# The second form of the attention rounds in a scan, attention and expert decoder layer: centred values, decays with the gate as bias, scores ahead of values

## What is computed

```python
log_fg = log_sigmoid(fg); cs = cumsum(log_fg)
log_D = where(lower triangle, cs - cs.T, -inf) + ig.T
D = exp(log_D - max(log_D))
C = (qh @ kh.T / sqrt(32)) * D
normalizer = maximum(abs(sum(C)), exp(-max_log_D))
h = (C / (normalizer + 1e-6)) @ vh
out = (h - mean(h)) * rsqrt(var(h) + 1e-5) * outnorm_scale     # over the 32 of a head
x = layernorm(x + out)
```

## Time and profile before

| | us |
|---|---|
| median of 3 runs | 702.19 |
| the three runs | 701.72, 706.64, 702.19 |
| the profiled execution | 706.54 |
| its span, first to last instruction | 704.9 |

### The profile page before, as it was taken

One profiled execution on the slowest core, in us unless ns is written; L12 is line 12 of the kernel. 1 busy time (PEld: TensorE's weight loads), 2 busy tenths in 40 slices (PEclk: granted clock), 3 DMA queues, 4 the chain that ended last, 5 costly groups with the idle time before them and its releaser, 6 DMA issues.

```text
span 704.9 us, 10813 instructions
## 1 busy us (share of the span) xinstructions
PE 544.6 (77%) x3387; PEld 386.7 (55%) x3387; DVE 430.6 (61%) x880; ACT 329.5 (47%) x732; POOL 369.7 (52%) x301
## 2 busy tenths in 40 slices
PE   2589999899889888686384889797878689989800
PEld 0234434445344447675263768686667568988800
DVE  1599999999999941676748376656352612211155
ACT  2475685876867553122132435444443323333327
POOL 1497979999789752216506163625253533322341
PEclk9999999999999995555555789998898899999955
DMA  4434535444454532732341735361616157788594
GB/s 148 148 101 148 175 122 166 146 170 167 137 179 146 191 74 52 133 62 62 77 113 42 193 120 158 136 232 36 203 63 216 59 177 243 241 292 270 170 244 117
DMA packets 83319, 104.51 MB, mean 148 GB/s; under 512 B 40784, under 2 KB 64592, under 8 KB 83136
## 3 DMA queue, kind: packets, MB, share of 16 engines
q1 hardware_dynamic: 74576, 90.99, 42.4%
q0 software_dynamic: 4320, 8.92, 3.7%
q10 hardware_dynamic: 4368, 3.93, 2.0%
HBM read 91.48 MB, written 12.34 MB: 147 GB/s over the span
## 4 chain that ended last, share of the span: by engine, by line
PE 25%; issue 24%; POOL 20%; DVE 10%; DMA 9%; ACT 3%; SPq 2%; another core or an unknown queue 1%; POOLq 0%; ACTq 0%; DVEq 0%
POOL hc L640 12%; PE pB L1063 7%; PE pq L1076 4%; DMA wslot<-in_expert_w 4%; PE py L818 4%; PE py L1063 2%; POOL y_dram L745 2%; PE pC L997 1%; ACT x_all L1457 1%; DMA y_dram<-dx,xin 1%; PE pa L979 1%; POOL xg_dram L736 1%; DMA x_all<-y_dram 1%; POOL bcs L604 1%
## 5 line engine op out<-in xcount | busy, mean ns | idle before, releaser
L640 POOL TENSOR_TENSOR hc<-h,Crep 128x1024 f32<-128x1024 f32 x64 | 149.7, 2356 | 14.6 <-DVE h L1507 13.2
L745 POOL DMA_INDIRECT y_dram<-dx,xin x71 | 68.9, 971 | 153.9 <-ACT dx L1378 144.8
L1063 PE MATMUL pB<-Crep,wslot 128*128 128x256 f32 (+1 forms) x556 | 118.9, 360 | 21.9 <-DMA wslot<-in_expert_w 10.7
L818 PE MATMUL py<-hc,ident 128*128 128x512 f32 x256 | 120.7, 598 | 8.1 <-POOL hc L640 8.1
L1063 PEld LDWEIGHTS pB<-Crep,wslot 128*128 128x128 f32 x556 | 90.8, 204 | 38.7 <-DMA wslot<-in_expert_w 14.0
L1498 DVE TENSOR_TENSOR u<-dx,pC 128x1024 f32<-128x1024 f32 x64 | 77.3, 1207 | 17.4 <-PE pC L807 17.3
L818 PEld LDWEIGHTS py<-hc,ident 128*128 128x128 f32 x256 | 46.8, 189 | 53.9 <-issue 37.4
L1789 DVE TENSOR_TENSOR Crep<-u,pB 128x512 f32<-128x512 f32 x35 | 24.0, 686 | 85.5 <-PE pB L1063 42.2
L1507 DVE TENSOR_TENSOR_SCAN h<-pB,u 128x1024 f32<-128x1024 f32 x32 | 73.1, 2285 | 1.0 <-ACT pB L1196 0.6
L1507 DVE TENSOR_TENSOR_SCAN h<-pa,u 128x1024 f32<-128x1024 f32 x32 | 73.1, 2284 | 0.0
L1789 DVE TENSOR_TENSOR u<-u,pB 128x512 f32<-128x512 f32 x36 | 24.8, 688 | 78.9 <-PE pB L1063 46.0
(11 more groups left out here) (225 smaller groups left out, 952.0 us busy)
## 6 DMA issues: line engine op xcount, KB each, us to landing
wslot<-in_expert_w SPq DMA_DIRECT2D x46, 768.0 KB
Crep<-c_dram SPq DMA_DIRECT2D x64, 512.0 KB, 3.8
h<-m_dram SPq DMA_DIRECT2D x16, 256.0 KB
xin<-xg_dram SPq DMA_DIRECT2D x25, 130.0 KB
cT_st<-in_ctx_T SPq DMA_DIRECT2D x8, 256.0 KB, 4.1
dx<-in_ctx_T SPq DMA_DIRECT2D x8, 256.0 KB, 4.0
delta<-in_ctx_tok SPq DMA_DIRECT2D x32, 64.0 KB
hc<-y_dram SPq DMA_DIRECT2D x8, 256.0 KB, 8.5
```

What stands on the lines that cost most here:

```text
L640: nc.gpsimd.tensor_tensor(hc[:, K % 4], h[:, K % 3], Crep[:, K % 4].rearrange("p a t -> p (a t)"), ALU.mult).then_inc(hc_done, 1)
L745: nc.gpsimd.indirect_dma_start(out=y2_dram, out_offset=bass.IndirectOffsetOnAxis(ap=xin[:, i % NX, a, D:D + 1].bitcast(i32), axis=0), in_= ...
L818: last = nc.tensor.matmul(py[:], ident[:], hc[:, K % 4, i * CH:(i + 1) * CH], start=False, stop=(K % STEPS == STEPS - 1 and i == 1))
L1063: last = nc.tensor.matmul(bank[:, o * a * P:(o + 1) * a * P], wslot[:, i % NW, stage * F + f * P:stage * F + (f + 1) * P], xgT[i % 2][:, 0 ...
```

## The change

1. Values are made on the chip: a matrix `hcenter` (identity minus 1/32 within each head's block), made on POOL in chunk 1 (`head_constants`), multiplies the keys on PE (`head_values`, four products of 128x128), so that values are centred by head; ACT copies them (`copy_values`). `load_v` goes.
2. `normalize` has no mean to subtract: two multiplies from PSUM by `outnorm` (part 0), the normalizer beside them, ACT squares from PSUM, the sum is multiplied twice by the normalizer's reciprocal, and one factor `vfac` scales the heads. The last subtraction and scaling moves from DVE to ACT (`normal_x2`).
3. For chunks 0 to 4 (`ADDED = 5`) the gates are no longer added on DVE; the exponential takes them as bias, in 16 instructions of 128x64. `weight_decay(c+2)` runs one round earlier than before, behind `copy_rows` (chunks below 5) or behind `normal_x2` (from 5, with `add_gates(c+2)` in round c).
4. Chunk 0's mask, decays, weights and values lie in `wslot`, so they are begun in the scan; `late(c)` picks the buffers.
5. In rounds below 5 (`FULL = 5`) `weights(c+1, 0)` and scores 2 and 3 are done earlier in the round, and POOL's `start_mask(c+2)` comes between the two halves of `send_rows`.
6. Logits and ranks lie in bank 1 of `pa` instead of `pC`. `turn_x2` waits for `ranks_read` instead of `x2T_copied`, and `logits` no longer waits for `hv_done`.

```diff
+            def head_constants():
+                nc.gpsimd.memset(hcenter[:], 0.0).then_inc(ones_set, 1)
+                for hh in range(H):
+                    nc.gpsimd.memset(hcenter[rows, rows], -1.0 / width).then_inc(ones_set, 1)
...
+                nc.gpsimd.tensor_tensor(hcenter[:], hcenter[:], ident[:], ALU.add).then_inc(ones_set, 1)
+                nc.gpsimd.memset(V1[0][:, :, S // 2:], 1.0).then_inc(ones_set, 1)
...
@@ POOL: scan and rounds
+                    if c + 1 == NCH and k == 6:
+                        start_mask(0)
...
-            start_mask(0)
             add_residual(NCH - 1)
             for c in range(-1, NCH + 1):
                 first = first_tiles(c)
                 if c >= 2:
                     send_rows(c - 2, 0)
+                if c < FULL and c + 2 < NCH:
+                    start_mask(c + 2)
                 scatters(first[0:1])
                 if c >= 2:
                     send_rows(c - 2, 1)
                 scatters(first[1:])
-                if c + 2 < NCH:
+                if c >= FULL and c + 2 < NCH:
                     start_mask(c + 2)
@@ SP
+                    if c + 1 == NCH and k == 1:
+                        load_heads(0)
+                    if c + 1 == NCH and k == 6:
+                        store_m(0)
+                    if c + 1 == NCH and k == 7:
+                        load_m(0)
...
-                if c + 2 < NCH:
-                    load_v(c + 2)
                 if c == 2:
                     store_m(1)
                     load_m(c + 3)
@@ PE
             sum_state(STEPS * NCH - 2)
+            head_values(0)
+            scores(0, 0)
+            scores(0, 1)
             sum_state(STEPS * NCH - 1)
             turn_m(0)
             center_y(NCH - 1)
-            scores(0, 0)
+            scores(0, 2)
+            scores(0, 3)
             variance(NCH - 1)
             turn_x1(NCH - 2)
-            scores(0, 1)
+            weighted_values(0, 0)
+            weighted_values(0, 1)
             project(NCH - 1)
             gate_products(NCH - 2)
-            scores(0, 2)
-            weighted_values(0, 0)
-            scores(0, 3)
-            weighted_values(0, 1)
@@ ACT
+                for m in range(TB * H):
+                    last = nc.scalar.activation(Dm[late(c)][:, m * S:(m + 1) * S], lmask[late(c)][:, m * S:(m + 1) * S], ACT.Exp,
+                                                bias=g_sb[:, c * TB * H + m:c * TB * H + m + 1])
...
+            def normal_x2(c):
+                act.wait_ge(x2_shift_done, c + 1)
+                act.wait_ge(z2_rstd_done, c + 1)
+                for b in range(TB):
+                    last = nc.scalar.activation(x2_rows(c)[:, b], z2[:, b], ACT.Identity, scale=rstd[:, b:b + 1],
+                                                bias=nma[:, b:b + 1])
...
                 if mid and c >= 4:
                     log_exp_table()
-                if front:
-                    weight_decay(c + 1)
                 if mid:
                     scale_heads(c)
+                if front:
+                    copy_values(c + 1)
                 expert_units(first[2:])
                 if back:
                     copy_rows(c - 1)
+                if c + 2 < ADDED:
+                    weight_decay(c + 2)
...
                 if mid:
                     z2_scale(c)
+                    normal_x2(c)
+                if ADDED <= c + 2 < NCH:
+                    weight_decay(c + 2)
                 expert_units(second[2:])
@@ DVE
-                mid(0)
-                if front:
-                    add_gates(c + 1)
-                mid(1, 2, 3, 4)
+                mid(0, 1, 2)
+                if front and c < FULL:
+                    weights(c + 1, 0)
+                rt(0)
+                mid(3, 4)
                 expert_units(first[0:1])
...
-                mid(8)
+                mid(8, 9)
                 rt(7)
-                if front:
+                mid(10)
+                if front and c >= FULL:
                     weights(c + 1, 1)
+                if ADDED <= c + 2 < NCH:
+                    add_gates(c + 2)
                 expert_units(second[0:1])
                 rt(8)
-                mid(9)
+                mid(11)
                 rt(9)
-                mid(10)
+                mid(12)
                 expert_units(second[1:2])
...
-                expert_units(second[2:3])
-                mid(13)
-                expert_units(second[3:])
+                expert_units(second[2:])
                 rt(17, 18, 19, 20)
```

More of the change, by code:

```diff
@@ L1122, in _ @@
                     logits(c - 1)
-                expert_units(first[1:3])
+                expert_units(first[1:2])
+                if front and c < FULL:
+                    scores(c + 1, 2)
+                    scores(c + 1, 3)
                 if front:
+                    head_values(c + 1)
+                expert_units(first[2:3])
+                if front and c >= FULL:
                     scores(c + 1, 2)
                 expert_units(first[3:])
+                if front and c >= FULL:
+                    scores(c + 1, 3)
                 if front:
-                    scores(c + 1, 3)
                     weighted_values(c + 1, 0)
@@ L1399, in _ @@
             copy_y(NCH - 1)
+            copy_values(0)
             normal_x1(NCH - 2)
@@ L1405, in _ @@
             floor_gates(0)
-            weight_decay(0)
+            weight_decay(1)
             z_squares(NCH - 1)
@@ L1845, in _ @@
             log_norm(0)
-            add_gates(0)
             weights(0, 0)
+            weights(0, 1)
             keep_gates(NCH - 2)
-            weights(0, 1)
             for c in range(0, NCH + 1):
```

289 lines of the change are left out of this document (162 added, 127 removed).

## The result

| | before | after |
|---|---|---|
| median, us | 701.96 (700.58 to 706.64, 4 runs) | 721.74 (716.91 to 725.23, 4 runs) |
| profiled execution, us | 706.54, span 704.9 | 716.91, span 715.2 |
| mean granted clock | 0.863 | 0.855 |

The changed kernel is slower: ratio 1.0246, 95% interval 1.0197 to 1.0295. One of all the executions in this document, the profiled one of run 3 (729.53 us), was disturbed, and it is left out of that run's median, of its ratio and of the table of rounds. The profiled execution is the fastest of its four runs; the spans differ by 10.3 us, the medians by 19.8.

What follows compares the result with a forecast made beforehand. No engine was taken as the bound throughout: DVE paces rounds without expert tiles, the cast-sends-weights-tile chain rounds 4 to 7. Terms 1.2 - 3 - 3 + 6.5 + 2.65 + 7 = +11.35 on 702.2 gave 713.5 us, range 690 to 722.

Steps and rivals of the forecast that it cites:

- Scan, start of round 0: Changeover to attention: chunk 6's gates row on DVE moves to about 281, round 0 starting with it, 3.3 us early.
- Decays 4.0: Chunk 0's decays on ACT: sixteen instructions with a bias take 4.0 us, +3.0 against the row they replace.
- The constants, forecast at 1.2: Scan, chunk 1: seven added POOL instructions of `head_constants` cost +1.2 us, from zero to 2.
- Rounds 1 and 2, -3: Rounds 1 and 2: less DVE work, partly offset by ACT and PE work, saves 1.5 us each, -3 together.
- Round 3, +6.5: Round 3: sends five to eight wait for the maxima and the mask, so tile 0 starts later; +6.5 us.
- Round 4, +2.65: Round 4: the mask stands between sends with its maxima long there, delaying the tile's weights; +2.65 us.
- Rounds 4 to 7, +7 for ScalarE's block: Rounds 4 to 7: `normal_x2` and decays between ACT's table loads add 2.4, 2.4, 1.3, 1.3 us; taken as +7.
- Round 7, +1.3, and the end, 0: Round 7: `normal_x2` between ACT's table loads adds 1.3 us; no term was given for the end.
- Rival A: Rounds 4 to 7: PE's wait for the DVE multiply at `logits` is the bound, so they shorten; 688.4 us, chance 0.20.
- Rival B: Rounds 0 to 2: TensorE keeps 2.4 GHz, 12 us less than the forecast; 701.5 us, chance 0.15.
- Rival C: Rounds 4 to 7: ACT's longer block is absorbed, 7 us less than the forecast; 706.5 us, chance 0.10.

Runs made afterwards that it cites:

- run 3: Changed kernel with only `turn_x2` and `copy_x2T` moved behind the first unit of a round; 722.12 us, ratio 1.0250.
- run 12: Kernel before, with the first tile's scatter behind all eight sends and, in rounds 5 and 6, the second head's scores behind the logits; 703.62 us, ratio 1.0025.
- run 10: Changed kernel with ScalarE's block emptied, `turn_x2` behind the first unit, second head's scores late in rounds 5 and 6; mask still between sends; 717.43 us.
- run 9: Changed kernel with mask behind the sends, `turn_x2` behind the first unit, second head's scores late in rounds 5 and 6; ScalarE's block kept; 704.81 us.
- run 1: Changed kernel with POOL's mask behind all eight sends in rounds 3 and 4; 718.07 us, ratio 1.0184.
- run 2: run 1 plus ScalarE's block emptied: `normal_x2` behind the last units, decays of chunks 5 to 7 where they stood before; 717.22 us, ratio 1.0176.
- run 11: run 6 plus the scatter of the first tile behind all eight sends; 687.30 us, ratio 0.9799 to the kernel before.
- the first edits: On the changed kernel: mask behind the sends, ScalarE's block emptied, `turn_x2` behind the first unit, second head's scores late; all together 703.66 us (run 6).
- the last one: The scatter of the first tile put behind all eight sends instead of between them; added to run 6 it gave 687.30 us.
- run 5: run 4 plus the scatter of the first tile behind all eight sends; 712.92 us, ratio 1.0132.
- run 7: run 1 plus the scatter of the first tile behind all eight sends, `turn_x2` still ahead of the first unit; 722.78 us, ratio 1.0264.
- run 4: run 2 plus the edit of run 3 (`turn_x2` and `copy_x2T` behind the first unit); 712.33 us, ratio 1.0139.
- run 6: run 4 plus, in rounds 5 and 6, the second head's scores moved from ahead of the logits to behind the centred values; 703.66 us, ratio 1.0007.
- run 8: Kernel before with only the scatter of the first tile put behind all eight sends; 701.51 us, ratio 0.9940.
- the third group's four: run 9, run 10, run 11 and run 12, measured on one chip beside the kernel before; 704.81, 717.43, 687.30 and 703.62 us.

## Why the prediction was right, and where it was not

Slower was right, and 721.7 lies within the range (690 to 722) by 0.3 us, 8.2 us above the 713.5 of the forecast. By the spans, +10.3 against +11.35 looks close, but that is luck: rounds 5 and 6 cost 13.2 us where the forecast gave them 3.7, and rounds 3, 4 and 7 and the end together came out 12.3 us below it.

- *Scan, start of round 0.* "Near 281" and "about 281" for the gates' row: 280.16 and 280.06. Decays 4.0: 3.92. Right. The 5.3 us that I had from the Trainium skill ("ScalarE: Activation LUTs", What ACT_TABLE_LOAD costs) left out what the same section says of neighbours, that they overlap by some 93 ns: with it sixteen come to an estimated 3.9, and the trace agrees (3.92). The constants, forecast at 1.2: the weighing behind them on POOL starts 1.45 us later (86.24 to 87.69), of which 0.5 is left at the scan's end (gates of chunk 5, 257.91 to 258.41).
- *Rounds 1 and 2, -3.* The lead is 4.1 us at the start of round 0, 1.2 at that of round 1 (303.04 to 301.81; forecast 1.8), 0.9 at that of round 2 and 3.6 at the store of the maxima (343.20 to 339.57; forecast 4.8). So round 0 gave back 2.9 us, where the forecast let a lead of 3.3 shrink to 3; round 1 gave nothing for -1.5, and the rest 2.7. The sum is near the forecast, by terms that are not. `head_values` was priced too low, at 1.1 us at 1.2 GHz and 0.65 at 2.4: eight passes take 2.08 and 1.05.
- *Round 3, +6.5.* The mechanism is shown: the wait between the sends is 5.59 us, and the tile starts at R + 21.7 for a forecast of R + 22. But the round grew by 3.0 only. The term assumed that the way from tile to cast stays, 14.0 us, less 0.5; it became 10.3. The profiled execution before had a hold in this round (3.26 us); in run 12, which is the kernel before up to the place of a scatter, and has no hold and asks for the weights at the same R + 9.6, the round is 30.3 us and the way from tile to cast 11.0, and against that the changed kernel is 6.3 longer, for a term of 6.5. The way is shorter since behind the tile's first eight matmuls the clock was at 2.4 GHz, where it had been at 1.2: groups of 1.13, 1.03 and 1.14 us for 2.07, 1.91 and 1.94, together 2.6; and the changed kernel has the four subtractions of L1650 (1.11) off VectorE's path. Run 10 against 9 has the whole term: 7.3.
- *Round 4, +2.65.* For the mask alone, 3.0 by run 1 and 3.4 by run 10 against 9: right, a little low. The whole round grew by 3.7, where the forecast had 5.05, with 2.4 of ScalarE's block.
- *Rounds 4 to 7, +7 for ScalarE's block.* The forecast gave 2.4 us in round 5 and 1.3 in round 6; the loads stand 2.0 us further apart in round 5 (4.86 for 2.88, `normal_x2` 1.65 and the decay 1.04 in them) and 1.0 in round 6 (488.74 to 492.65). But rounds 5 and 6 grew by 6.7 and 6.5. This is the step that failed: the term took ScalarE's block at its own length, with the clock as before, and put "the wait of `turn_x2` for `ranks_read` (about 1.2)" into slack. The block makes TensorE wait 2.3 us for `weigh`, and the first unit of the next round then runs at 1.2 GHz; with the wait at `turn_x2` it also starts behind the cast. Both delay `weigh`, and with it a scatter and four sends, and so the rows come 1.4 us later. Either one taken away undoes that (weights asked for at 16.0 in run 2, 16.1 in run 3, for 18.2). And the waits cost more than their length. In round 5 a 2.46 us wait for rows is followed by work at 1.2 GHz: from that `turn_x` to the next it takes 13.1 us (430.53 to 443.62), against 8.6 for the same work before (426.80 to 435.41): +4.5. From there to the third `turn_x` it is 8.5 against 6.5, ScalarE's block: +2.0. With 0.6 up to the first and -0.4 behind the third, that is the 6.7.
- *Round 7, +1.3, and the end, 0.* Measured -1.2 and -5.0; round 8 +0.2. Behind the last cast TensorE waits 2.8 us for weights instead of 6.4, which is 3.6 of the 5.0; no run tested why.
- *Rival A* (rounds 4 to 7 give back the wait at `logits`). The wait did vanish and the rounds did not shorten, as forecast. Yet it was the nearest to what the change could be worth: with the new stalls mended, run 11 has rounds 5 and 6 3.4 to 3.6 us shorter than before and 687.3 us, for the 688.4 of A; run 12, the kernel before with two of the edits, has nothing of it. That number's match is in part chance, since A counted no scatter.
- *Rival B.* The clock from 284 to 340 us is 0.50. Refuted. *Rival C.* Absorbed while another stall stands (run 2: 0.8 us; 1.5 in rounds 5 to 8 of run 10 against 9). With the scatter moved it is not: run 9 lacks both, and 2.5 us of block and 4.0 of clock are its whole distance to run 11 in round 5.

The medians differ by 9.5 us more than the spans, since the profiled execution was the fastest of four after, and 4.6 us above the median before. Which rounds vary from execution to execution was not traced.

## What to carry to other kernels

Where several stalls share one slack, price them by undoing all but one: by the ratios, each of the first edits here gave between -6 and 9 us, and the last one, worth nothing or less in runs 5 and 7, was worth 16.7 us in rounds 5 to 8 once the others stood; from the changed kernel to run 11 it is 31 us. When a wait is added ahead of dense TensorE work, look for the work behind it that then runs at 1.2 GHz, and add it: it was 4.5 us behind the wait for rows here, beside the wait itself, and in the kernel before some 3 and 1.6 us behind its waits of 3.42 and 3.49 at `logits`. And put nothing that waits, no mask and no scatter, between the transfers that the next stage's weights hang on.

## What the runs showed of the hardware that was not expected

- *The hold.* While GpSimd issues its indirect transfers 1.26 us apart, instructions that wait for TensorE alone start late, on VectorE and ScalarE at once: the copy of the logits 6.8 to 10.2 us after the matmuls' end in the profile, in rounds 5 and 6 of runs 2 to 5 and 7. In all ten of these the copy starts 0.6 to 2.1 us behind the end of the last transfer of the series, in eight of them 1.9 to 2.1; no run shortened the series, so whether its end is the release was not tested.
  Moving 16 matmuls on 32 rows from ahead of the logits to behind brought the copy to 1.6 us in run 6, left holds of 5 to 6.5 us at later instructions, and took 8.7 us off the time. The hold was in the profiles of the first two groups of runs, in short forms in both kernels (3.26 and 3.51 us), and in none of the third group's four.
  The order of work does not explain that: runs 8 and 12 have the same order up to round 4, and run 8 has holds of 4.48 and 3.25 us in rounds 2 and 3 and run 12 has none; runs 6 and 10 have the same order from round 5 on, and run 6 has holds of 5.04 and 6.54 there and run 10 none. What is left is the chip, or something else that varies between executions; why it happens stays open.
- *The clock after short waits.* Behind waits of 2.3 to 3.0 us in otherwise dense work (the changed kernel, runs 9 and 10), and in round 6 of run 9 behind one of 1.31 us, matmuls ran at 1.2 GHz (eight matmuls of `up` in 3.78 us for 1.99), and the clock stayed at 2.4 GHz all through rounds 5 and 6 of run 11, where no wait was over 0.91 us. That a wait is the cause is inferred from this contrast; no run added a wait alone.
